# The choice of experts in one block by halves, the latents' norm next to their sums, and the pair weights loaded earlier

## The reference, cut to what matters

```python
    hidden = resid + (ctx @ o_w + o_b)
    xt = layer_norm(hidden, ln2_w, ln2_b).reshape(T, D)
    logits = xt @ router_w
    probs = jax.nn.softmax(logits, axis=-1)
    top1 = jnp.argmax(probs, axis=-1)
    m1 = jax.nn.one_hot(top1, E)
    top2 = jnp.argmax(jnp.where(m1 > 0, -jnp.inf, logits), axis=-1)
    m2 = jax.nn.one_hot(top2, E)
    loc1 = jnp.cumsum(m1, axis=0) - 1.0
    loc2 = jnp.cumsum(m2, axis=0) - 1.0 + m1.sum(axis=0, keepdims=True)
    m1 = m1 * (loc1 < C); m2 = m2 * (loc2 < C)          # C = 128 places in each of 16 experts
    ...  # the kept tokens' rows go to their experts; two weights for each token
    x = x + resid + moe_out
    # second layer
    lat = layer_norm(layer_norm_plain(x), ln2_w, ln2_b) * (1.0 + scale) + shift
    q = lat @ Wq.T ; k, v = split(concat(norm(ctx), lat) @ Wkv.T)   # 16 heads of 64
```

## Time and profile before

| | us |
|---|---|
| median of 3 runs | 3514.93 (3513.35 to 3516.91) |
| the profiled execution | 3514.66 |
| its span, first to last instruction | 3512.9 |
| PE busy in the span | 3179.4 |
| DVE busy | 2469.1 |
| ACT busy | 1696.7 |
| POOL busy | 1890.1 |

### The profile page before, as it was taken

One profiled execution on the slowest core, in us unless ns is written; L12 is line 12 of the kernel. 1 busy time (PEld: TensorE's weight loads), 2 busy tenths in 40 slices (PEclk: granted clock), 3 DMA queues, 4 the chain that ended last, 5 costly groups with the idle time before them and its releaser, 6 DMA issues. The chain is left out here.

```text
span 3512.9 us, 50949 instructions
## 1 busy us (share of the span) xinstructions
PE 3179.4 (91%) x18448; PEld 1857.0 (53%) x18448; DVE 2469.1 (70%) x4319; ACT 1696.7 (48%) x2063; POOL 1890.1 (54%) x1174
## 2 busy tenths in 40 slices
PE   5979798586348999999999999999999999999998
PEld 3757576232324555555555555555555555555445
DVE  6979798653248776877777777787777778767523
ACT  5758576243124445444444444444444444544442
POOL 3857576111233655655665565565566556556670
PEclk8989898567679999999999999999999999999998
DMA  1000000000310000000000000000000000000001
GB/s 62 1 1 1 1 1 1 12 1 1 129 33 3 1 1 1 4 1 1 4 1 1 1 4 1 1 4 1 1 1 4 1 1 2 1 1 1 1 1 35
DMA packets 20600, 28.47 MB, mean 8 GB/s; under 512 B 5124, under 2 KB 12424, under 8 KB 20232
## 3 DMA queue, kind: packets, MB, share of 16 engines
q1 hardware_dynamic: 19016, 22.09, 1.9%
q0 software_dynamic: 1344, 3.15, 0.3%
HBM read 21.56 MB, written 3.67 MB: 7 GB/s over the span
## 5 line engine op out<-in xcount | busy, mean ns | idle before, releaser
L2068 ACT ACTIVATE pair_probs<-banks 128x1024 f32<-128x1024 f32 (+1 forms) x944 | 965.5, 1026 | 1035.1 <-PE banks L1976 983.6
L2121 DVE TENSOR_REDUCE pair_peaks<-banks 128x1 f32<-128x512 f32 (+1 forms) x1800 | 1086.2, 666 | 271.0 <-PE banks L1958 257.4
L2214 POOL TENSOR_TENSOR pair_total_pool<-pair_total_pool,pair_probs 128x1536 f32<-128x1536 f32 x208 | 724.5, 3483 | 754.7 <-DVE pair_total L2135 749.4
L1999 PE MATMUL banks<-pair_probs,pair_values 128*64 128x512 f32 (+1 forms) x3776 | 872.5, 600 | 0.0
L1958 PE MATMUL banks<-pair_k_high,pair_q_high 64*128 64x512 f32 (+1 forms) x1920 | 566.8, 441 | 19.8 <-DVE pair_peaks L2114 10.3
L2203 POOL TENSOR_TENSOR pair_total_pool<-pair_total_pool,pair_probs 128x1024 f32<-128x1024 f32 x224 | 536.0, 2393 | 37.9 <-POOL pair_total_pool L2214 21.7
L2135 DVE TENSOR_TENSOR pair_total<-pair_total,pair_probs 128x512 f32<-128x512 f32 (+2 forms) x464 | 457.1, 985 | 95.1 <-ACT pair_probs L2068 70.3
L1999 PEld LDWEIGHTS banks<-pair_probs,pair_values 128*64 128x64 f32 (+1 forms) x3776 | 248.3, 136 | 472.4 <-issue 384.5
L1976 PE MATMUL banks<-pair_q_shift,pair_one_rows 64*128 64x512 f32 (+1 forms) x1888 | 475.5, 396 | 3.1 <-ACT pair_probs L2068 3.1
L1958 PEld LDWEIGHTS banks<-pair_k_high,pair_q_high 64*128 64x128 f32 x1920 | 262.3, 184 | 349.1 <-issue 202.7
L1976 PE MATMUL banks<-pair_q_high,pair_k_high 64*128 64x512 f32 (+1 forms) x1888 | 426.9, 391 | 0.0
(11 more groups left out here) (325 smaller groups left out, 3801.5 us busy)
## 6 DMA issues: line engine op xcount, KB each, us to landing
expert_w<-in_fc SPq DMA_DIRECT2D x32, 256.0 KB, 3.6
context_rows<-in_ctx SPq DMA_DIRECT2D x10, 320.0 KB, 6.7
dense_w<-in_We SPq DMA_DIRECT2D x2, 1024.0 KB, 9.3
experts_in<-expert_zeros SPq DMA_DIRECT2D x1, 1024.0 KB, 3.8
expert_b<-in_fc_b SPq DMA_DIRECT2D x2, 512.0 KB, 4.9
expert_rows<-experts_in SPq DMA_DIRECT2D x16, 64.0 KB, 1.9
experts_out<-expert_result POOLq DMA_DIRECT2D x4, 256.0 KB, 4.1
row_parameters<-in_rows SPq DMA_DIRECT2D x1, 896.0 KB, 8.8
```

Of the source, the lines that this page charges most:

```text
L1999: last = pe.matmul(out[heads[head], :], values[0:n, ring_of(h // 2, i // 4), i % 4, heads[head]], probs_of(h, i)[0:n, head, :], start=i == ...
L2068: act.activation(probs_of(h, i)[0:n], slot(e)[0:n], ACT.Exp, scale=1.0 / 8.0).then_inc(S["expd"].sem, 1)
L2121: v.reduce_max(peaks[:, head, t, b:b + 1], fill_bank(f, head)[:, 0:width(b)], axis=AX).then_inc(S["peaked"].sem, 1)
L2214: pool.tensor_tensor(pooled[:], pooled[:], three, ALU.add).then_inc(S["pooled"].sem, 1)
```

## The change

The blocks from the turning of the attention's rows to the addresses become one block, `choose_experts`. It works by halves of four tiles: projection, residual and norm of half 0, then of half 1; the transposes, the copies (now all on ACT) and the logits of each half; then the choice of each half on DVE. The norm works tile by tile with `scalar_tensor_tensor` (mean and gain in one instruction, root and shift in the next). In many places only the last instruction of a group is waited for. The place in an expert is compared and multiplied straight from the counting bank. What only the gather and the combination need (gather addresses, weights) goes to `weigh_choices`, in the first block of `sixteen_experts`.

In the second block of `sixteen_experts`, the statistics of each tile of x are taken right behind its sum, the root on POOL of the first half stands between the gathers of tile 6 and tile 7, and the norm, transposes and the scaled copies (ACT, with the modulation folded into scale and shift beforehand) end the block. `latents_turned` goes. The first two pairs' weights have tiles of their own from the start, and their 12 loads stand on SP behind the experts' loads. The clearing of the two small tiles moves to the front of DVE's list in the main block of the attention, with a wait on PE before each half's first scores. In the diff, lines of "..." leave out the bodies of the removed functions, declarations and counts.

```diff
-def layernorm_rows(k, src, dst, gain=None, shift=None, twice=False):
...
-def transpose_rows(k, src, dst, gain=None, shift=None):
...
-def project_rows(k, src, w, take):
...
-def route(k, xt, xtT, router, weights, scatter, gather):
...
+def choose_experts(k, context, turned, hidden, normed, router, T):
...
+    with k.nc.Block() as block:
+        @block.tensor
+        def _(pe):
+            for t in range(TT):
+                pe.transpose(k.ps[:, t // 4, t % 4 * P:(t % 4 + 1) * P], context[:, t, :],
+                             k.ident[:]).then_inc(S["turned"].sem, 1)
+            for h in range(2):
+                wait(pe, "kept", h + 1)
+                for t in halves[h]:
+                    pe.matmul(k.ps[:, 2 + h, t % 4 * P:(t % 4 + 1) * P], turned[:, t * P:(t + 1) * P],
+                              k.square("L0_ffn_o_w"), start=True, stop=True).then_inc(S["projected"].sem, 1)
+            pe.wait_ge(k.sig("router_loaded").sem, 16)
+            for h in range(2):
+                wait(pe, "normed", h + 1)
+                for t in halves[h]:
+                    pe.transpose(k.ps[:, 4 + h, t % 4 * P:(t % 4 + 1) * P], normed[:, t, :],
+                                 k.ident[:]).then_inc(S["normed_turned"].sem, 1)
+                wait(pe, "normed_kept", h + 1)
+                for t in halves[h]:
+                    pe.matmul(logit_banks[h][:, t % 4 * E0:(t % 4 + 1) * E0], turned[:, t * P:(t + 1) * P], router[:],
+                              start=True, stop=True).then_inc(S["routed"].sem, 1)
+            wait(pe, "chosen", 2)
+            pe.matmul(located, upper[:], flat(chosen[:]), start=True, stop=False)
+            wait(pe, "counted", 1)
+            pe.matmul(located, k.ones[:], flat(before[:, 0:TT, :]), start=False, stop=True).then_inc(S["located"].sem, 1)
+
+        @block.scalar
+        def _(act):
+            for h in range(2):
+                wait(act, "turned", 4 * h + 4)
+                act.activation(turned[:, columns[h]], k.ps[:, h, :], ACT.Copy).then_inc(S["kept"].sem, 1)
+            for h in range(2):
+                wait(act, "normed_turned", 4 * h + 4)
+                act.activation(turned[:, columns[h]], k.ps[:, 4 + h, :], ACT.Copy).then_inc(S["normed_kept"].sem, 1)
+            for h in range(2):
+                wait(act, "lowered", h + 1)
+                act.activation(probs[:, tiles[h], :], probs[:, tiles[h], :], ACT.Exp).then_inc(S["expd"].sem, 1)
+
+        @block.vector
+        def _(v):
+            def norm(h):
+                wait(v, "projected", 4 * h + 4)
+                keep(k, v, v.tensor_tensor(flat(hidden[:, tiles[h], :]), flat(hidden[:, tiles[h], :]), k.ps[:, 2 + h, :],
+                                           ALU.add))
+                for t in halves[h]:
+                    last = v.bn_stats(k.bn[:, t, :], hidden[:, t, :])
+                keep(k, v, last)
+                for t in halves[h]:
+                    last = v.bn_aggr(k.moments[:, t, :], k.bn[:, t, :])
+                keep(k, v, last)
+                v.tensor_scalar(k.moments[:, tiles[h], 1], k.moments[:, tiles[h], 1], EPS, None,
+                                ALU.add).then_inc(S["varied"].sem, 1)
+                for t in halves[h]:
+                    last = v.scalar_tensor_tensor(normed[:, t, :], hidden[:, t, :], k.moments[:, t, 0:1],
+                                                  k.row("L0_ffn_ln2_w"), ALU.subtract, ALU.mult)
+                keep(k, v, last)
+                wait(v, "rooted", h + 1)
+                for t in halves[h]:
+                    last = v.scalar_tensor_tensor(normed[:, t, :], normed[:, t, :], k.stat[:, 2, t:t + 1],
+                                                  k.row("L0_ffn_ln2_b"), ALU.mult, ALU.add)
+                last.then_inc(S["normed"].sem, 1)
+
+            def choose(h):
+                wait(v, "routed", 4 * h + 4)
+                keep(k, v, v.tensor_copy(flat(logits[:, tiles[h], :]), logit_banks[h]))
+                for t in halves[h]:
+                    last = v.max(best[:, t, :], logits[:, t, :])
+                keep(k, v, last)
+                for t in halves[h]:
+                    last = v.max_index(place[:, t, :], best[:, t, :], logits[:, t, :])
+                keep(k, v, last)
+                keep(k, v, v.tensor_copy(placef[:, tiles[h], :], place[:, tiles[h], 0:2]))
+                    last = v.tensor_tensor(chosen[:, tiles[h], n * E0:(n + 1) * E0],
+                                           expert[:].unsqueeze(1).to_broadcast([P, 4, E0]),
+                                           placef[:, tiles[h], n:n + 1].to_broadcast([P, 4, E0]), ALU.is_equal)
+                last.then_inc(S["chosen"].sem, 1)
+                v.tensor_tensor(probs[:, tiles[h], :], logits[:, tiles[h], :],
+                                best[:, tiles[h], 0:1].to_broadcast([P, 4, E0]),
+                                ALU.subtract).then_inc(S["lowered"].sem, 1)
+                wait(v, "chosen", h + 1)
+                for t in halves[h]:
+
+            keep(k, v, v.memset(before[:, 0, :], 0.0))
+            wait(v, "constants", 4)
+            for h in range(2):
+                norm(h)
+            for h in range(2):
+                choose(h)
+            v.tensor_tensor(before[:, 0:TT, E0:2 * E0], before[:, 0:TT, E0:2 * E0],
+                            before[:, TT:TT + 1, 0:E0].to_broadcast([P, TT, E0]), ALU.add).then_inc(S["counted"].sem, 1)
+
+            keep(k, v, v.tensor_scalar(flat(first[:]), flat(placef[:]), float(CAP), None, ALU.mult))
+            keep(k, v, v.tensor_tensor(ahead[:], first[:], spare[:], ALU.subtract))
+            wait(v, "expd", 2)
+            keep(k, v, v.reduce_sum(total[:].squeeze(2), probs[:], axis=AX))
+            keep(k, v, v.reciprocal(total[:], total[:]))
+            keep(k, v, v.tensor_tensor(probs[:], probs[:], total[:].to_broadcast([P, TT, E0]), ALU.mult))
+
+            wait(v, "located", 1)
+            keep(k, v, v.scalar_tensor_tensor(out=flat(chosen[:]), in0=located, scalar=float(CAP + 1), in1=flat(chosen[:]),
+                                              op0=ALU.is_lt, op1=ALU.mult))
+            keep(k, v, v.scalar_tensor_tensor(out=flat(product[:]), in0=located, scalar=-1.0, in1=flat(chosen[:]),
+                                              op0=ALU.add, op1=ALU.mult))
+            v.reduce_sum(kept[:], both(chosen), axis=AX)
+            keep(k, v, v.reduce_sum(slot[:], both(product), axis=AX))
+            keep(k, v, v.tensor_tensor(ahead[:], ahead[:], kept[:], ALU.mult))
+            keep(k, v, v.tensor_tensor(ahead[:], ahead[:], slot[:], ALU.add))
+            keep(k, v, v.tensor_tensor(ahead[:], ahead[:], spare[:], ALU.add))
+            keep(k, v, v.tensor_copy(T["scatter"][:], ahead[:]))
+
...
+            for h in range(2):
+                wait(pool, "varied", h + 1)
+                pool.tensor_tensor(k.stat[:, 2, tiles[h]], k.moments[:, tiles[h], 1], k.half[:, 0:4],
+                                   ALU.pow).then_inc(S["rooted"].sem, 1)
...
+def weigh_choices(k, v, T):
...
+    keep(k, v, v.tensor_tensor(first[:], first[:], kept[:], ALU.mult))
+    keep(k, v, v.tensor_tensor(first[:], first[:], slot[:], ALU.add))
+    keep(k, v, v.tensor_copy(T["gather"][:], first[:]))
+    for n in range(2):
+        last = v.tensor_tensor(product[:, :, n * E0:(n + 1) * E0], probs[:], chosen[:, :, n * E0:(n + 1) * E0], ALU.mult)
+    keep(k, v, last)
+    keep(k, v, v.reduce_sum(weights[:], both(product), axis=AX))
+    keep(k, v, v.tensor_tensor(total[:], weights[:, :, 0:1], weights[:, :, 1:2], ALU.add))
+    keep(k, v, v.tensor_scalar(total[:], total[:], float(2.0 ** -23), None, ALU.max))
+    keep(k, v, v.reciprocal(total[:], total[:]))
+    keep(k, v, v.tensor_tensor(weights[:], weights[:], total[:].to_broadcast([P, TT, 2]), ALU.mult))
...
+def load_pair(k, A, sp, g):
...
+    for tile, name, n, cols in ((wq, "wq", 2 * g, heads[0]), (wq, "wq", 2 * g + 1, heads[1]),
+                                (wk, "wk", g, slice(0, P)), (wv, "wv", g, slice(0, P))):
+        sp.dma_start(tile[:, g % 2, cols], A[name][n, :, cols]) \
+          .then_inc(k.sig(("pair_weights_even", "pair_weights_odd")[g % 2], True).sem, 16)
+def load_pair_output(k, A, sp, g):
...
+    for n, head in enumerate((slice(0, HD1), slice(HD1, P))):
+        sp.dma_start(wo[head, g % 2, :], A["wo"][2 * g + n, head, :]) \
+          .then_inc(k.sig(("pair_wo_even", "pair_wo_odd")[g % 2], True).sem, 16)
...
             def _(v):
+                weigh_choices(k, v, T)
+                modulation = k.stat[:, 0, 2:3]
+                keep(k, v, v.tensor_scalar(modulation, k.col("cond_1024"), 1.0, None, ALU.add))
+                keep(k, v, v.tensor_tensor(latent_scale, k.col("L1_xcond_ln2_w"), modulation, ALU.mult))
+                keep(k, v, v.tensor_scalar(latent_shift, k.col("L1_xcond_ln2_b"), modulation, k.col("cond_1024"), ALU.mult,
+                                           ALU.add))
```

(54 more changed lines are left out.)

264 lines of the change are left out of this document (51 added, 213 removed).

## The result

| | before | changed |
|---|---|---|
| median, us | 3514.38 (3513.35 to 3516.91, 4 runs) | 3490.68 (3485.40 to 3492.07, 4 runs) |
| ratio | | 0.9924, 95% interval 0.9909 to 0.994 |
| profiled execution | 3514.66, span 3512.9 | 3485.40, span 3483.7 |

The changed kernel is 23.7 us faster by these medians, against 27.5 forecast. Its median lies 3.4 us above the forecast of 3487.3, inside the stated range of 3484 to 3492 but outside the band of 3485.5 to 3489.5 that had 0.60 of the chances. It was run again twice beside the experiments: 3487.85 against 3516.03 (5 and 10 runs, 28.2 less), and 3489.04 against 3515.72 (5 and 9 runs, 26.7 less). Both of these medians lie in the band.

A forecast was written before the change was run, and what follows sets the result against it. No engine bounds the two rewritten stages, only one chain running between engines. Gains 16.4 + 11.3 - 0.2 = 27.5 off 3514.66 give 3487.2, forecast as 3487.3; band 3485.5 to 3489.5 (0.60), bounds 3484 to 3492.

The forecast's parts named there:

- The first stretch: First transpose to first scatter, the choice of experts: 16.4 us less than the 41.60 before.
- step 5: Tile sum 0.32 and softmax work 1.27 us on DVE; counting product ends 0.1 us earlier, so DVE sets the time.
- Waits left out: DVE norm and choice of half 1: if unwaited instructions save nothing, 1.5 and 0.9 us more, 2.4 together.
- The rule weighed against them: The Trainium skill's statement that leaving out semaphores between DVE instructions saves nothing; by it the gain shrinks by 2.4 us.
- The rival that they don't overlap: Choice of experts: PE's and ACT's work of both halves stays on the chain, 3.65 + 1.7 us more, 3492.6; chance 0.05.
- The rival on the slower side: DVE's moved work holds up POOL's scatters, up to 3.2 us each; all 15 others give 3536; chance 0.01.
- the rival that both pairs are held up: POOL's roots in both stretches cost 1.5 us more, part of the dearer pieces case (to 3492), chance 0.20.
- 2.67: Time in us of the power on POOL at L153 beside DVE's large instructions, taken as a possible held-up root.
- a collision with the store: Pair loads share engines with the last store: +0.2 us taken, rival up to 3.4, giving 3490.5; chance 0.05.
- The second stretch: Last tile's sum to first query product: 6.77 us plus 0.6 block end, 11.3 less than before.
- The rival put an early rise down to the transposes: PE's clock rises earlier behind the first query product, up to 3 us less, about 3485.3; chance 0.08.
- The signs: Expected in the profile: first scatter at 882 to 884, query product 26 to 29 us earlier, root 1.0 to 1.3 us.

The follow-up runs named there:

- all_waited: The changed kernel with a wait behind every DVE instruction of the norm halves and of the maxima and searches: 3491.52 us.
- norms_first: The changed kernel with PE's transposes of half 0 waiting for both norm halves: 3494.27 us.
- keys_later: The changed kernel with both roots behind the gathers and the keys' scaling moved from beside POOL's scatters to DVE's wait for the first expert: 3483.05 us.
- front_only: The changed kernel with only the choice of experts in one block, norm of latents, pair loads and memsets as before: 3498.40 us.
- tail_only: The changed kernel with only the new end, the choice of experts in its old blocks: 3503.84 us.
- roots_last: The changed kernel with the first half's root behind all 16 gathers on POOL: 3488.03 us.

## Why the prediction was right, by its steps

**The first stretch** was forecast as 25.2 us, and is 25.26 to 25.28 where the clock was 0.50. The steps are less exact than their sum. From the first transpose to the first residual it took 3.98 us at that clock, against 3.71: the forecast's half projection of 1.70 is half of 3.41, and in that trace the clock was 0.50 up to 862.0 but 0.65 on the mean from there to the end of the projection; all 16 products take 3.78 at 0.50. The other steps hardly hang on the clock, and in the first trace are these: both norms 9.11 against 9.28 (the first 4.48 against 4.64, DVE waiting 0.18 for the root and not 0.25); half 1 through PE, ACT and PE 3.80 against 3.65, with DVE idle for 1.05 us of it and not 0.6; the choice 2.92 against 3.05; the sums and softmax 1.69 against 1.59; the addresses 2.49 against 2.6; block end to scatter 1.27 against 1.26. These errors of 0.1 to 0.3 us have both signs and cancel to 0.1, which is luck. In step 5 the wrong engine was named: the counting product ended 0.10 us behind DVE, not DVE 0.1 us behind it. And the sum left out that transposes and projection can run at either clock, 1.4 us less in two of the ten traces with the new front.

**Waits left out** were priced from the rows, at 2.4 us for part of them; waiting for all costs 3.75 (all_waited). The rule weighed against them would have been wrong here by all of that.

**Halves.** The rival that they don't overlap was priced at 3.65 + 1.7. norms_first takes out what the 3.65 stand for and measures 3.6. The 1.7, the projection of half 1, was not tested. In the traces those products do run beside DVE's first norm: in the second trace of the changed kernel they end at 861.46, and DVE had begun at 859.89.

**The weights beside the scatters** cost nothing visible: scatters 24.2 and 24.3 us in the changed kernel, 24.1 and 23.6 before. The short instructions held none: the second scatter, beside the weights, took 0.96, and that is the price of an unheld one, not the 1.24 of the first. The rival on the slower side is wrong for the moved work. What holds one scatter is DVE's long work, before and after alike: 3.5 us in the first traces of both kernels, 0.7 of it beside the sum and 2.8 beside the scaling, which keys_later takes away.

**The roots** took 1.03 and 1.04 us in the first stretch and 1.06 twice in the second, so the rival that both pairs are held up falls. Its price was also too low by the prediction's own rows: 1.3 us more for each root of the first stretch and 3.2 for the second come to 5.8, where it counts 1.5. And 2.67 was no measure for 128x4: the size counts too, since a power over 128x8 with no large two-input instruction beside it took 1.64 (L207, at 622.38 in the trace before).

**The loads of the pairs** were forecast at +0.2 for a collision with the store. The store did take 3.00 us instead of 2.79, but it does so in kernels without the early loads as well. The term was of the right size by luck, for a reason that was not the one given; which part of the change brings the 0.2 stays open, as front_only and tail_only both have it. The 12 loads took SP 6.3 us (949.10 to 955.41) and not 4.9, and were still all issued 1.1 us before the store.

**The second stretch** was forecast as 6.77 + 0.6 = 7.37, of which 1.05 is the root ahead of the last gathers; behind the last sum that leaves 6.32, and it is 6.31. The block end cost 0.54 and not 0.6. The root ahead of the last gathers cost 0.7 to 0.9 (roots_last) and not 1.05.

**The clock** behind the first query product rose early in some traces and late in others, of both kernels. The rival put an early rise down to the transposes, which now end 1.35 us before the first product. But the first and third traces of the changed kernel are at 0.50 throughout the 8 us, and front_only and the second trace of the kernel before, with the old end, rise early. So as a gain of the change the rival is not borne out, though its size was about right: an early rise is worth 1.5 to 2.1 us, where it counted 2. It is a spread that the forecast should have had on both kernels; what decides it stays open.

**The signs.** The first scatter stood at 879.23 and not at 882 to 884, and the first query product 29.9 us earlier and not 26 to 29. Of that, 2.15 us are the first transpose, which stood earlier for reasons ahead of the changed stretch, and 1.4 the clock; in the other two traces of the changed kernel the query product came 28.1 and 26.0 earlier. The root between the gathers of tiles 6 and 7 took 1.06, four maxima 0.41, and the first query product waits for no DMA, as forecast.

The measured gain of 23.7 in the first comparison, 28.2 and 26.7 in the others, brackets the 27.5. The sum over the seven points is 27.0 less (means 162.1 and 135.1 of two and three traces). Single pairs of those traces differ by 25.3 to 28.7, so part of the half microsecond between forecast and mean is luck as well. Where the untraced executions spent their difference is not known, as they have no lengths of stages. The sum itself gives 3514.93 - 27.5 = 3487.4; the forecast wrote 3487.3.
